# Two buffers for the negative side of the NF4 levels, used by pieces of weights in turns

## What is computed

```python
def _L1_ffn_ref(x, q_weight, q_scale, bias, lora_A, lora_B):
    w = NF4_LEVELS[q_weight].reshape(-1, GROUP_SIZE) * q_scale[:, None]
    w = w.reshape(OUT, IN).astype(x.dtype)
    base = jnp.einsum('bsi,oi->bso', x, w) + bias
    lora = jnp.einsum('bsr,or->bso', jnp.einsum('bsi,ri->bsr', x, lora_A), lora_B)
    return base + SCALING * lora
...
x = x + _L0_ffn_ref(_L0_cond_ref(x, itok_B_0_15, L0_cond_weights), L0_ffn_w, L0_ffn_b)
x = x + _L1_ffn_ref(_L1_cond_ref(x, L1_cond_weights, itok_B_0_15), L1_ffn_q_weight, L1_ffn_q_scale, L1_ffn_bias, L1_ffn_lora_A, L1_ffn_lora_B)
```

## Time and profile before

| | |
|---|---|
| median of 3 runs | 342.19 us (341.97 to 342.35) |
| the profiled execution | 340.92 us, of which the span is 338.9 us |
| granted TensorE clock in the span | 1.0 |
| busy: PE, DVE, ACT, POOL | 98%, 69%, 49%, 72% |
| chain that ended last | PE 78%, POOL 6%, issue 5%, SPq 4%, DVE 4% |

### The profile page before, as it was taken

One profiled execution on the slowest core, in us unless ns is written; L12 is line 12 of the kernel. 1 busy time (PEld: TensorE's weight loads), 2 busy tenths in 40 slices (PEclk: granted clock), 3 DMA queues, 4 the chain that ended last, 5 costly groups with the idle time before them and its releaser, 6 DMA issues.

```text
span 338.9 us, 8207 instructions
## 1 busy us (share of the span) xinstructions
PE 330.8 (98%) x3150; PEld 270.8 (80%) x3150; DVE 234.5 (69%) x358; ACT 164.4 (49%) x300; POOL 243.3 (72%) x158
## 2 busy tenths in 40 slices
PE   8999998999999999999999999999999999999996
PEld 8768776878888888887878888888888888888884
DVE  6889877999999999969895826246262462724623
ACT  2799668869877877847451405014041140411400
POOL 0379995997887995966999966677466774667742
PEclk9999999999999999999999999999999999999999
DMA  6996611654354345301000151503315024150302
GB/s 223 307 340 175 195 33 31 251 192 158 106 181 162 100 154 165 130 11 64 6 0 3 70 188 67 191 4 124 131 68 193 2 116 142 66 189 5 126 31 93
DMA packets 25800, 40.60 MB, mean 120 GB/s; under 512 B 7810, under 2 KB 16002, under 8 KB 25762
## 3 DMA queue, kind: packets, MB, share of 16 engines
q1 hardware_dynamic: 25090, 39.48, 34.1%
q10 hardware_dynamic: 672, 0.61, 0.6%
HBM read 25.40 MB, written 14.68 MB: 118 GB/s over the span
## 4 chain that ended last, share of the span: by engine, by line
PE 78%; POOL 6%; issue 5%; SPq 4%; DVE 4%; DMA 2%; ACT 1%; POOLq 0%; DVEq 0%
PE acc L1305 45%; PE acc L1261 22%; PE xT L1205 3%; PE xT L1187 3%; PE spare L1187 2%; POOL x_first L609 2%; SPq L478 2%; DMA bias<-in_L_ffn_b 2%; PE acc L1337 2%; POOL x_first L616 1%; PE acc L1339 1%; SPq L472 1%; POOL side_p L643 1%; DVE hl L932 1%; SPq L470 1%
## 5 line engine op out<-in xcount | busy, mean ns | idle before, releaser
L1305 PE MATMUL acc<-W,hh 128*128 128x512 f32 x256 | 81.4, 389 | 0.0
L1261 PE MATMUL acc<-T,hh 128*128 128x512 f32 x192 | 76.5, 398 | 0.0
L1261 PE MATMUL acc<-T,hl 128*128 128x512 f32 x192 | 75.1, 391 | 0.0
L609 POOL TENSOR_TENSOR X<-X,bias 128x1024 f32<-128x1024 f32 x28 | 68.6, 2449 | 0.0
L780 ACT ACTIVATE spare<-q_raw 128x512 f32<-128x512 int32 x96 | 56.1, 600 | 17.4 <-DVE side_n L988 6.2
L1074 DVE TENSOR_TENSOR X<-X,acc 128x512 f32<-128x512 f32 x48 | 32.9, 685 | 39.4 <-PE acc L1305 29.2
L1305 PEld LDWEIGHTS acc<-W,hh 128*128 128x128 f32 x256 | 48.1, 188 | 10.0
L668 POOL TENSOR_TENSOR X<-X,ys 128x512 f32<-128x512 f32 x24 | 30.2, 1286 | 33.3 <-DVE ys L1063 33.2
L1305 PE MATMUL acc<-W,hl 128*128 128x512 f32 x128 | 49.8, 389 | 0.0
L815 ACT ACTIVATE hh<-xT 128x512 fp32r<-128x512 f32 x16 | 8.7, 596 | 81.8 <-PE xT L1187 81.8
L1261 PEld LDWEIGHTS acc<-T,hh 128*128 128x128 f32 x192 | 36.1, 188 | 8.0
(11 more groups left out here) (102 smaller groups left out, 602.3 us busy)
## 6 DMA issues: line engine op xcount, KB each, us to landing
out<-X SPq DMA_DIRECT2D x22, 512.0 KB, 3.1
X<-in_x SPq DMA_DIRECT2D x12, 512.0 KB, 3.3
X<-out SPq DMA_DIRECT2D x12, 512.0 KB, 3.6
q_raw<-in_L_ffn_q_weight SPq DMA_DIRECT2D x16, 256.0 KB, 2.9
w_in<-in_L_ffn_w SPq DMA_DIRECT2D x14, 256.0 KB, 5.6
x_first<-in_x SPq DMA_DIRECT2D x4, 512.0 KB, 4.4
out<-x_first SPq DMA_DIRECT2D x4, 512.0 KB, 5.0
out<-X SPq DMA_DIRECT2D x4, 256.0 KB, 2.0
```

The costliest lines, as they stand in the source:

```text
L609: pool.tensor_tensor(x_of(g), x_of(g), bias[:, :], ALU.add).then_inc(s_xb, 1)
L1261: mm = pe.matmul(acc[:, bank_of(q), :], a[:, k, :], T0[:, n, k, :], start=(k == 0 and j == 0), stop=(k == KB - 1 and j == 1))
L1305: mm = pe.matmul(acc[:, bank, :], a[:, k, :], w1(part, c, k), start=(k == 0 and j == 0), stop=(k == HB - 1 and j == len(terms) - 1))
```

## The change

`side_n` gets two buffers of 512 columns, and piece d uses buffer d % 2: in the line that writes it first, in the three maxima and in the subtraction. The wait of ScalarE ahead of that line is for the subtraction of piece d - 2 instead of that of piece d - 1. All tensors that lie behind `side_n` in SBUF move by 2 KB in each partition. Counts and order of the instructions stay.

```diff
-        side_n = sb("side_n", [P, BANK], F32)
+        side_n = sb("side_n", [P, 2, BANK], F32)
...
-                pool.tensor_tensor(lev, lev, side_n[:, :], ALU.subtract).then_inc(s_lev, 1)
+                pool.tensor_tensor(lev, lev, side_n[:, d % 2, :], ALU.subtract).then_inc(s_lev, 1)
...
-                        need(act, s_lev, d)
-                        dst = side_n[:, :]
+                        need(act, s_lev, d - 1)
+                        dst = side_n[:, d % 2, :]
...
-                    dst = side_n[:, :] if sign else side_p[:, d % SP, :]
+                    dst = side_n[:, d % 2, :] if sign else side_p[:, d % SP, :]
```

## The result

The changed kernel took 339.38 us (median; 339.29 to 339.74) against 342.15 us (341.97 to 342.35, four executions now) for the kernel before. Three executions of the later runs were far longer (368 and 1870 us for the kernel before, 664 us in e9), and the ratios and ranges leave them out.

What follows compares the result with a forecast made beforehand. TensorE, busy 330.8 of 338.9 us, was taken to wait for VectorE between 53 and 70 us. Turns 0 and 1 gave 0.78 + 0.86 = 1.64, turn 3 brought 2.08: 342.19 - 2.08 = 340.1 us, range 339.6 to 341.6.

Steps and rivals of the forecast that it cites:

- The first wait: ScalarE's 2.25 us wait for GpSimd's subtraction at piece 1, ending at 43.18: becomes a wait for TensorE, worth 0.
- maximum 15: VectorE's maximum on piece 2's negative side: starts at 50.74 instead of 52.82 us, 2.08 us earlier.
- The turns 0 and 1: TensorE's stalls at the first two turns of weight pieces: 0.78 and 0.86 us lost, all won, 1.64 in sum.
- turn 3: TensorE's turn waiting for a sum of blocks: starts at 68.01 instead of 70.09, 0.21 us of wait left, gain 2.08.
- The slower rival at the third product: Second block: GpSimd's chain meets VectorE's L1022 more often, at most 3.4 us lost, giving 343.5 us; chance 0.04.
- The move of the tensors: Tensors behind side_n shifted by 2 KB: costed at nothing, 0.3 us either way at most.
- The freed instructions of VectorE: VectorE's work from 50.7 to 52.8 us beside GpSimd, second input in PSUM: runs free, price nothing.
- signs of being wrong: The prediction is wrong if turn 3 starts later than 68.5, or a stage behind 70 us is longer than before.
- from the profiled execution to the median: Profiled execution lies 1.27 us under the median; the same 2.08 us was taken off 342.19, giving 340.1 us.
- the second wait: ScalarE's 2.20 us wait for GpSimd's subtraction at piece 2, ending at 51.67: removing it puts VectorE 2.08 us ahead.
- The range: 339.6 to 341.6 us, to hold the forecast and the partial case, chance 0.80 together.
- the forecast's own 0.25 us of margins: ScalarE loses some 0.25 us at tile 6's mix; if that came through, VectorE's advance would be 1.8 us.

Runs made afterwards that it cites:

- e9: Changed kernel with the first block's bias load issued ahead of the last four pieces of w: 339.27 us, ratio 0.9917.
- e3: Kernel before with room for two buffers of side_n, only the first used, and the old wait: 341.56 us, ratio 0.9991.
- after: The changed kernel itself, two buffers and both waits eased, as first measured and profiled: 339.38 us, ratio 0.9902.
- e2: Changed kernel with two buffers, but only ScalarE's wait at piece 2 eased: 340.42 us, ratio 0.9965.
- e5: Changed kernel with one more GpSimd addition of 128 x 512 ahead of the weights of piece 1: 339.22 us, ratio 0.9927.
- e10: Changed kernel run again without edit, for a larger sample and a second profile: 339.84 us, ratio 0.9923.
- before: The kernel before, one buffer, in its recorded profile: 340.92 us, where its timed runs had a median of 342.15 us.
- e7: Changed kernel with VectorE's low_x(0, 0) ahead of ternary(0, 0) at the start: 339.57 us, ratio 0.9935.
- e12: Kernel before, one buffer, GpSimd taking piece 1's weights ahead of add_bias(4) and result_half(5), and piece 0's ahead of lora_A's low part: 339.38 us, ratio 0.9916.
- e0: Kernel before, unchanged, run once more with a profile: 341.78 us, against 341.80 us beside it.
- e6: Kernel before, one buffer, with GpSimd taking the weights of piece 1 ahead of add_bias(4) and result_half(5): 340.11 us, ratio 0.995.
- e8: Kernel before with the first block's bias load issued ahead of the last four pieces of w: 342.69 us, ratio 1.0022.
- e1: Changed kernel with two buffers, but only ScalarE's wait at piece 1 eased: 342.35 us, ratio 1.0009.

## Why the prediction was right and where it was wrong

**The mechanism, by its steps: right.** The first wait became one for TensorE. VectorE's maximum 15 is 2.09 us earlier in the chain of tile 4 (2.08 forecast). The turns 0 and 1 have no wait. At turn 3 the transposes start 0.37 us after the last matmul's start. An unhindered turn takes 0.23, as turn 2 of the kernel before, whose last matmul started at 64.86:

```profile
65.09 0.60 PE L1337 MATMUL acc<-ident,side_p 128*128 128x128 f32 x4
```

So 0.14 us is left (0.21 forecast). The slower rival at the third product did not happen: 0.21 us there, against 0.24. The move of the tensors wins nothing (e3). The freed instructions of VectorE kept their 0.68 us beside GpSimd.

Two of the prediction's signs of being wrong did come up. Turn 3 started at 68.60, after the 68.5 that it named. That is the later start: counted from tile 4's mix it comes after 68.60 - 44.30 = 24.30 us instead of 70.09 - 43.69 = 26.40, 2.10 less. And one stage behind 70 us is longer, by the 0.33 us at 126.8. This wait stands in after, e2, e5 and e10, and with 0.2 us in e3, but not in before, e7, e9 and e12; its cause is open.

**The step that failed: from the profiled execution to the median.** The text carried the 1.27 us between them over unchanged (342.19 - 2.08). That assumes that what makes a usual run longer is as long after the change. 0.7 us of it were in the first wait, which the change removes too. The kernel before: median 342.15, profile 340.92, so 1.23 us. With the upper group of the table, a span 1.2 us longer means a subtraction at 51.5 instead of 50.33; e0's lay at 51.35. The changed kernel: forecast 338.84 for the profiled execution, measured median 339.38, 0.54 us more. The gain is thus 2.08 + 1.23 - 0.54 = 2.77 us. The rows of e0 give the same without any median: 0.67 us for the split of tile 4 and 7.27 - 5.18 = 2.09 us from there to maximum 15, together 2.76. The profile of after shows where such a remainder lies: its span is 1.0 us above the forecast 336.8, of which 0.6 us are the later start and 0.3 us the wait at 126.8. e9, whose profile has no such wait at 126.8 us, had a span of 337.1. In the twelve profiles that keep the order of the loads, that of the bias is issued at 17.4 to 18.3 us and takes 7.9 to 10.1 us to land. So most of the difference arises on the way and not at the issue. What makes it was not tested.

**The same step as a term of the sum: the first wait was mis-sized.** I took 0, from rows where ScalarE still waited 0.62 us for TensorE after it. That margin is small beside the spread of GpSimd's start: in the ten other profiles that keep the first part of the order, its first addition came between 0.0 and 2.2 us later than the 25.71 of the recorded one, 1.1 in the middle. In a usual run the late lines, not TensorE's mix, decide when tile 4 is split (e0: `side_n` line at 44.19, split at 45.25 without a wait). The differences e2 to after (0.6 to 1.0 us) and e6 to e12 (0.7 us) are its worth once the second wait is gone. It is the part 1.23 - 0.54 = 0.69 us of the difference above, not on top. The forecast of the second wait, 2.08 us, was right to 0.01.

**The range** was built from the forecast's own 0.25 us of margins and the spread of three runs (0.4 us). Larger samples of the kernel before spread over 340.66 to 344.02. The distance of the profiled execution from them, 1 us below the lowest of the three, should have been read as a term of unknown place. Put wholly into the removed wait it gives 342.19 - 2.08 - 1.27 = 338.8, which would have been the lower end.

## What to carry to other kernels

When the profiled execution is outside the timed runs, the difference is a duration with a place. Ask which wait would hold it, and whether the change removes that wait; both ends belong in the range. A buffer that is freed by an engine with a long queue ties everyone to that queue's start, here to the landing of one load 24.6 us earlier. Such a tie can be cut by a second buffer or by moving the release forward in the queue, and e12 got the same time without memory. A wait worth nothing in one trace is so only by the margin of what ends next, here 0.6 us. Before moving a load forward, look at what its first user will then run beside (e8).

## What the runs showed of the hardware

The landing of the first block's bias, behind 14 loads of w on the same queue, varied between executions: 7.9 to 10.1 us after its issue. GpSimd's first addition of it started between 25.69 and 27.87 us in profiles whose start differs in nothing. From there to the subtraction of piece 1 GpSimd's queue took 24.6 to 24.8 us each time in the kernels that keep its order (51.35 - 26.73 in e0, 51.59 - 26.95 in after), 1.0 us more with the added instruction. An addition of 128 x 512 with both inputs from the same tensor took 1.04 us on GpSimd, against 1.3 us for the usual ones of that size. A VectorE addition with both inputs in SBUF took 2.28 and 2.09 us where GpSimd's addition of the bias had started before it (e8, e9), and 0.69 us alone; VectorE's instructions with one input in PSUM kept 0.68 to 0.69 us beside GpSimd. After 2.44 and 1.91 us in which TensorE stood still (e1, e8) its granted clock was at 0.50 and 0.53 between 58 and 60 us and back at 1.00 from 62 us on.
